# A graph network kernel on one core: the first message step placed inside the building of the adjacency

## The reference

```python
def gnn(node_feats, W1, b1, W2, b2, W_ih, b_ih, W_hh, b_hh, src, dst):   # 3125 nodes, 256 features
    for _ in range(6):                                                   # NUM_STEPS
        h = relu(node_feats @ W1.T + b1) @ W2.T + b2
        msg = segment_sum(h[src], dst, num_segments=3125)                # 53125 edges, sorted by dst
        gx = msg @ W_ih.T + b_ih
        gh = node_feats @ W_hh.T + b_hh
        xr, xz, xn = split(gx, 3); hr, hz, hn = split(gh, 3)
        r = sigmoid(xr + hr); z = sigmoid(xz + hz); n = tanh(xn + r * hn)
        node_feats = (1 - z) * n + z * node_feats
    return node_feats

def reference(x, src, dst, ...):
    x = x + gnn(layernorm(x), ...)
    x = x + ffn(layernorm(x))            # 8 experts, top 2 by gate, 256 -> 512 -> 256
    return x
```

## Time and profile before

| | us |
|---|---|
| median of 3 runs (2141.41 to 2143.67) | 2142.3 |
| the profiled execution | 2137.68 |
| its span | 2135.8 |
| preparation, 0 to the first build instruction | 129.2 |
| build, seven turns | 129.2 to 333.4 |
| flag, eleven relu sums, entry of the step loop | 333.4 to 371.7 |
| the rest of step 0, to the first message matmul of step 1 | 371.7 to 626.1 |
| steps 1 to 5 and the last stage | 626.1 to 2135.8 |

### The profile page before, as it was taken

How to read it: one execution, slowest core, us unless ns; L and a number is a source line. 1 busy time by engine, 2 the same in 40 slices (tenths; PEclk the granted TensorE clock), 3 DMA queues, 4 the chain that set the end, 5 groups by cost and what they waited for, 6 DMA issues and landing times.

```text
span 2135.8 us, 31987 instructions
## 1 busy us (share of the span) xinstructions
PE 1899.5 (89%) x11128; PEld 1125.1 (53%) x11129; DVE 1108.7 (52%) x2621; ACT 598.2 (28%) x1297; POOL 346.7 (16%) x454
## 2 busy tenths in 40 slices
PE   1666766999999999999999999999999999947996
PEld 1533334444564456544574445644466455637996
DVE  6579993245443445334452344524453355654775
ACT  0145553112221222221232122312222111215664
POOL 1012224555000000000000000000000011342665
PEclk7679998999999999999999999999999999968998
DMA  9910003443000000000000000000000010293543
GB/s 271 336 29 0 0 0 131 139 143 124 1 2 1 1 1 1 2 1 1 1 1 2 1 1 1 2 1 1 1 1 1 3 36 33 80 368 61 84 72 58
DMA packets 73647, 106.08 MB, mean 50 GB/s; under 512 B 11742, under 2 KB 64777, under 8 KB 72484
## 3 DMA queue, kind: packets, MB, share of 16 engines
q1 hardware_dynamic: 50238, 46.09, 7.1%
q0 software_dynamic: 18368, 38.09, 7.0%
q10 hardware_dynamic: 4902, 20.01, 2.4%
HBM read 43.59 MB, written 61.77 MB: 49 GB/s over the span
## 4 chain that ended last, share of the span: by engine, by line
PE 63%; issue 14%; DVE 13%; POOL 7%; ACT 1%; ACTq 0%; POOLq 0%; DMA 0%; SPq 0%; DVEq 0%
PE bank L1398 33%; PE bank L1422 23%; DVE hot_key L757 6%; PE bank L1382 4%; POOL out L559 3%; DVE hot_row L751 2%; POOL slot_in L536 2%; POOL tick L558 1%; PE bank L1377 1%; PE bank L1296 1%; PE bank L1324 0%; DVE r_lo L817 0%; PE bank L1270 0%; DVE st L643 0%; DVE xa L678 0%
## 5 line engine op out<-in xcount | busy, mean ns | idle before, releaser
L1398 PE MATMUL bank<-adj,r_hi 128*128 128x512 fp8e4 (+2 forms) x2100 | 730.9, 353 | 0.0
L1398 PE MATMUL bank<-adj,r_lo 128*128 128x512 fp8e4 (+2 forms) x2100 | 730.8, 353 | 0.0
L1398 PEld LDWEIGHTS bank<-adj,r_hi 128*128 128x128 f16 x2100 | 205.9, 98 | 190.0 <-issue 1.9
L1398 PEld LDWEIGHTS bank<-adj,r_lo 128*128 128x128 f16 x2100 | 205.7, 98 | 189.8 <-issue 1.8
L824 DVE SCALAR_TENSOR_TENSOR m_lo<-bank,msg_unit,m_hi 128x512 f16<-128x512 f32 (+2 forms) x84 | 57.2, 682 | 304.6 <-ACT m_hi L1109 304.6
L1324 PE MATMUL bank<-hot_key,hot_row 128*128 128x400 f16 x588 | 139.0, 351 | 60.5 <-DVE hot_key L757 58.1
L523 POOL MEMSET x_rows<- 128x4 f32 (+1 forms) x3 | 0.2, 98 | 1126.4 <-PE bank L1499 1126.4
L1422 PE MATMUL bank<-m_hi,wct_hi 128*128 128x512 f16 (+2 forms) x504 | 177.3, 352 | 0.0
L1422 PE MATMUL bank<-m_lo,wct_hi 128*128 128x512 f16 (+2 forms) x504 | 177.3, 352 | 0.0
L1422 PE MATMUL bank<-m_hi,wct_lo 128*128 128x512 f16 (+2 forms) x504 | 177.3, 352 | 0.0
L1422 PE MATMUL bank<-x_hi,wht_lo 128*128 128x512 f16 (+2 forms) x504 | 177.3, 352 | 0.0
(11 more groups left out here) (295 smaller groups left out, 3011.2 us busy)
## 6 DMA issues: line engine op xcount, KB each, us to landing
slot_in<-fill_rows SPq DMA_DIRECT2D x2, 13520.0 KB, 69.1
ffn_scratch<-pair POOLq DMA_DIRECT2D x32, 512.0 KB, 3.2
ffn_w<-ffn_scratch ACTq DMA_DIRECT2D x8, 2048.0 KB, 19.3
x_rows<-in_L_ffn_W POOLq DMA_DIRECT2D x32, 256.0 KB, 3.9
slot_x<-slot_in SPq DMA_DIRECT2D x30, 260.0 KB, 3.3
xa<-in_x SPq DMA_DIRECT2D x1, 3072.0 KB
x<-in_x ACTq DMA_DIRECT2D x1, 3072.0 KB
out<-x SPq DMA_DIRECT2D x4, 512.0 KB
```

Source lines behind the costliest of these rows:

```text
L1398: last = mm(bank[f][:, 0:n], r[:, q, f * P:(f + 1) * P], c, start=q == 0 and i == 0, stop=q == NT - 1 and i == len(todo) - 1)
```

## The change

The build loop is written out in full on all engines, and step 0 is worked beside it: window w of step 0 is now turn w's 448 columns (the last has 438). While turn w+1 is built, PE also runs the messages of window w; while turn w+2 is built, the gates of window w. The relu sums of step 0 stand in turns 0 and 1. To have banks for this, the slices use two banks (`RING` = 2) instead of four, and the degree sums take a place in the same ring. The 196 small matmuls of line 1328, the register work of the loop and the copies of `turn_key` go; DVE waits on `slice_full` itself. The window 5 gates, window 6 and eleven relu sums of step 1 follow the build, and the flag is read behind them. If the flag is set, x is restored and step 0 is done again with the exact counts; for that SP writes `x_hi` and `x_lo` to DRAM (2 x 1.6 MB, `x_kept`) before ACT's first eviction may run. In the preparation the slot sums come right behind `picked`, ahead of the weights; six parts of x stand ahead of the combined weights and seven between the eight groups of turned weights.

```diff
-RING = 4
+RING = 2
+X_EARLY = 6
+TURN_COLS = GROUP * SW
+FUSED_COL = [w * TURN_COLS for w in range(NW)]
+FUSED_LEN = [min(TURN_COLS, N + N % 2 - c) for c in FUSED_COL]
+CHUNK_Q = (0, 4, 8, 12, 16, 19, 22, NT)
@@ SP
+            sp.wait_ge(sem("state_lo"), NW)
+            for i, half_x in enumerate((x_hi, x_lo)):
+                sp.dma_start(x_kept[i], half_x[:].rearrange("p t n -> p (t n)")).then_inc(sem("x_kept"), 16)
@@ DVE: gate_op(s, w, f, k) is one of the nine gate operations
+            def beside(w, b):
+                if w == -1 and b % 3 == 1 and b >= 4:
+                    relu_lo(b // 3 - 1, b // 3 - 1, first=True)
...
+                if w >= 1 and b == 2:
+                    msg_lo(FIRST, w - 1, 1)
+                if w >= 2 and b == 3:
+                    state_lo(FIRST, w - 2)
+                if w >= 0 and b == 17:
+                    msg_lo(FIRST, w, 0)
+                for f, places in enumerate(((6, 8, 9, 10, 10, 13, 13, 14, 14), (18, 20, 21, 22, 22, 25, 25, 26, 26))):
+                    if w >= 1 and b in places:
+                        for k in range(GATE_OPS):
+                            if places[k] == b:
+                                gate_op(FIRST, w - 1, f, k)
+            for g in range(NSL):
+                hots(g)
...
+                beside(g // GROUP - 1, g % GROUP)
@@ ACT
+            act.wait_ge(sem("x_kept"), 32)
+            for g in range(NSL):
+                evict(g)
+                beside(g // GROUP - 1, g % GROUP)
@@ PE
+            def beside(w, b):
+                if w == -1 and b % 3 == 0 and b // 3 < RELU_BUILD:
+                    relu_sum(FIRST, b // 3)
+                if w == 0 and b in (0, 2, 4, 6):
+                    relu_sum(FIRST, RELU_BUILD + b // 2)
+                for f, places in enumerate(((2, 4, 5, 6), (14, 16, 17, 18))):
+                    if w >= 1 and b in places:
+                        gate_sum(FIRST, w - 1, f, places.index(b))
+                for f in range(DT):
+                    c = b - 7 - 12 * f
+                    if w >= 0 and 0 <= c < 7:
+                        messages(FIRST, w, f, CHUNK_Q[c], CHUNK_Q[c + 1], False)
+
+            for g in range(NSL):
+                slice_sums(g)
+                beside(g // GROUP - 1, g % GROUP)
+                if g % GROUP == GROUP - 1:
+                    degree_sums(g // GROUP)
+            gates(FIRST, NW - 2, 0)
+            messages(FIRST, NW - 1, 0, 0, NT, False)
+            gates(FIRST, NW - 2, 1)
+            messages(FIRST, NW - 1, 1, 0, NT, False)
...
+            for u in range(FUSED_A):
+                relu_sum(SECOND, u)
+            gates(FIRST, NW - 1, 0)
+            for u in range(FUSED_A, FUSED_B):
+                relu_sum(SECOND, u)
+            gates(FIRST, NW - 1, 1)
+            for u in range(FUSED_B, FILL_B):
+                relu_sum(SECOND, u)
             slow = read_slow_flag(pe)
...
-                with pe.Fori(0, LAST) as s:
+                with pe.Fori(1, LAST) as s:
```

More of the change, by code:

```diff
@@ L862, in state_lo @@
[L862 to L870 removed]
+                v.memset(small[:, 1:2], 0.0).then_inc(sem("re_gate_ops"), LEAD)
+                for u in range(USES):
+                    relu_lo(u, u, "re_")
@@ L871, in _ @@
+                for u in range(FILL_B):
+                    relu_lo(USES + u, u, "re_")
+            v.memset(small[:, 0:1], 0.0).then_inc(sem("build_over"), 1)
+            with dve.Fori(1, LAST) as s:
                 for u in range(FILL_B, USES):
@@ L1081, in _ @@
+            gates(FIRST, NW - 1, 1)
+            state_hi(FIRST, NW - 1)
+            for u in range(FUSED_B, FILL_B):
+                relu_hi(USES + u, u)
             slow = read_slow_flag(act)
@@ new lines, in messages @@
+            def messages(s, w, f, q0, q1, exact, again=""):
+                n, c0 = columns_of(s, w, again)
+                fused = s is FIRST and not again
+                if fused and q0 == 0:
+                    pe.wait_ge(sem("stage_free"), GROUP // 2 * (w + 1))
+                    if w:
+                        pe.wait_ge(sem("msg_lo"), half(s, w - 1, f) + 1)
+                if fused and w == 0:
+                    pe.wait_ge(sem("relu_lo"), (q1 + 1) // 2)
+                if not fused and w == 1 and f == 0:
+                    pe.wait_ge(sem(again + "msg_lo"), half(s, 0, 0) + 1)
+                    mm(bank[0][:, 0:2], ones_h[:], b1_rows[:, 0:2], start=True, stop=True)
+                if exact:
+                    pe.wait_ge(sem("planes_in"), (s + 1) * (32 * NW) + 32 * (w + 1))
+                for q in range(q0, q1):
+                    counts = [planes[:, i, q, 0:n] for i in range(2)] if exact else [adj[:, q, c0:c0 + n]]
+                    todo = [(r, c) for c in counts for r in (r_hi, r_lo)]
+                    for i, (r, c) in enumerate(todo):
+                        last = mm(bank[f][:, 0:n], r[:, q, f * P:(f + 1) * P], c,
+                                  start=q == 0 and i == 0, stop=q == NT - 1 and i == len(todo) - 1)
+                if q1 == NT:
+                    last.then_inc(sem(again + "msg_sums"), 1)
@@ new lines, in gates, with slice_sums @@
+            def gates(s, w, f, again=""):
+                for k in range(4):
+                    gate_sum(s, w, f, k, again)
+            def slice_sums(g):
+                i, b = divmod(g, GROUP)
+                ring_free(pe, g + i)
+                pe.wait_ge(sem("hots_full"), g + 1)
+                for s in range(SLOTS):
+                    k = (b % DEEP) * SLOTS + s
+                    last = mm(bank[2 + (g + i) % RING][:, 0:NT * SW], hot_row[b // 2 % 2][:, b % 2, s, :], hot_key[k][:], start=s == 0, stop=s == SLOTS - 1)
+                last.then_inc(sem("slice_full"), 1)
```

597 lines of the change are left out of this document (352 added, 245 removed).

## The result

| | before | after |
|---|---|---|
| median of 4 runs (lowest to highest), us | 2141.86 (2140.48 to 2143.67) | 2045.05 (2044.29 to 2045.87) |
| profiled execution: time, span, us | 2137.7, 2135.8 | 2045.75, 2043.7 |
| PE busy, share of the span | 89% | 91% |

The ratio is 0.9548 [0.9531, 0.9564], 96.8 us less by the medians. 2050 was forecast, 5 us too much.

What follows compares the result with a forecast made beforehand. DVE was taken to bound the build and PE the steps. Step 1 moving from 626.1 to 534.4 saves 91.7 us: 2137.7 becomes 2046.0, plus 4.6 for the median, said as 2050; range 2033 to 2072, chance 0.68.

Steps and rivals of the forecast that it cites:

- What bounds each stage, and that a step's matmuls fit beside the build: DVE bounds a build turn (28.7 of 29.0 us), PE a step (250 of 254), so step matmuls fit beside the build.
- Unit prices: Costs per operation: a 448-column matmul 0.189 us, a relu sum 1.5, a DVE gate operation 0.62 to 0.70, an eviction 0.49.
- Slot sums early: Preparation: slot sums right behind `picked` end at 64 us, DVE reaches its wait at 63.8, so they cost nothing there.
- State of x: Preparation: `state_lo` done at 111 us instead of 128.7, with 6 us for seven interleaved parts; ends 105 and 118.
- Copy of x: Before ACT's first eviction: queue held by the fill until 111, 10.5 us of copy, there at 124; ends 120 and 132.
- Turn 0 and 1: First two build turns: PE ends the first at 156.5 us, the second at 197.5, with 39.1 of matmuls and 2 more.
- rival 1: Fused turns: DVE's in-order waits cost 10 us a turn, making a turn 57 us and the result 2085; chance 0.18.
- Turns 2 to 6: Fused turns: PE paces with 47.4 us, stalls 1.7 at the turn's seam and 0.9 elsewhere, 50 a turn; ends 47.4 and 55.
- Tail: From the last slice to step 1: gates, messages, relu sums, last `state_lo`, then 4.6 and 6.8 us of branch; 84.1 us.
- Clock at the start of step 1: At step 1's start: 7 us without PE work make the clock fall again, costing 2.8 us.
- The sum: Whole kernel: step 1 starts 91.7 us earlier, so 2046.0 us profiled; 4.6 more for the median, stated as 2050.
- The clock in the fused turns: Fused turns: a quarter of PE's work at half speed makes a turn 50 + 12 us, 2110 in all; chance 0.05.

Runs made afterwards that it cites:

- TensorE's extra work: Changed kernel with the twelve 448-column matmuls of the first gate sum run twice in each of turns 2 to 6: 2053.4 us, ratio 0.9591.
- the kernel without any jump: Changed kernel with TensorE's program lacking the flag, the redo of step 0 and the steps with exact counts: 2050.2 us, ratio 0.9576.
- the kernel that jumps early: Changed kernel with TensorE reading the flag and jumping over the redo before step 1's eleventh relu sum, not behind it: 2043.1 us, ratio 0.9542.

## Why the prediction was right, step by step

- **What bounds each stage, and that a step's matmuls fit beside the build:** right, and shown from both sides (2.26 of 2.27 us for TensorE's extra work, nothing for DVE's).
- **Unit prices:** right; 448 columns at 0.189 gave 2.27 and the turn grew by 2.26.
- **Slot sums early:** 64 forecast, 64.0 measured; DVE waited 0.5 us for them.
- **State of x:** 111 forecast, 105.35 measured. The term that was mis-sized is the seven interleaved parts, 6 us. From the combined weights to the last part it took 22.1 us (83.2 to 105.35) where the block alone had taken 20.1: the parts cost 2. The other 1.8 us are in what stands ahead (83.2 against 85.0). It cost the forecast nothing, because the copy lands no earlier.
- **Copy of x:** first eviction forecast at 124, measured at 123.6, for the reason given: the fill held the queue (to 112, forecast 111). The bytes went at 420 to 440 GB/s, not at 311, and landing took some 3.5 us (from about 120 to 123.4) where 2 were allowed for issue and landing together: two errors that cancelled, so the 0.4 us are luck.
- **Turn 0 and 1:** ends at 156.5 and 197.5 forecast, 156.7 and 199.7 measured; turn 1 was 2.0 us under-priced (43.0 against 41). Its matmuls are the 39.1 worked out, and PE stood for 3.9 us: 2.6 in the middle, where 2 were forecast, and the rest at its first slices and before its degree sums, for which nothing was set. In the middle PE waited 1.9 us for `hot_key`, which stood on DVE behind `m_lo`, which had waited 1.3 us for ScalarE's `m_hi`. That is rival 1's mechanism, once and small.
- **Turns 2 to 6:** 50 forecast, 48.84 measured, 5.8 us in all. The matmuls are the 47.4 worked out plus 0.5; stalls were priced at 2.6 (1.7 at the seam, 0.9 for the rest) and are 0.9 to 1 in all.
- **Tail:** 84.1 forecast, 82.4 measured (443.9 to 526.3), but made of other parts. The step that failed is the branch: I added the 4.6 us of the flag and the 6.8 of the loop entry from the earlier trace rows as two separate delays. With no work between them they are one, 6.3 us, as the kernel without any jump shows. Against that, up to the last `state_lo` it took 2 us more, and the eleventh sum 3.1 instead of 1.8 us, each of its 256-column matmuls 0.21 apart as at 1.2 GHz. Most of the 2 us has the same cause, which the forecast set at nothing here: behind a wait of 2.4 us for `r_lo` a whole relu sum ran at half the clock, 3.0 us instead of 1.5 (the window below).
- **Clock at the start of step 1:** 2.8 forecast, 2.0 measured (24.5 us to the mark where it was 22.5), granted clock 0.91 in that stretch. In the kernel that jumps early it is 1.00 there, and the stretch takes 22.5.
- **The sum:** steps 1 to 5 would start 91.7 us earlier, with step 1's loss in it; they did so by 97.8. The 6 us are the seam (5.8 us), the double jump (5.1) and the clock (0.8), less turn 0 (0.2), turn 1 (2.0) and what the tail took more before the jump (3.4). The profile's last stage then took 5.6 more than before, by scatter, and hid most of it; the medians show it. The working's 2046.0 for the profiled execution, where 2045.75 was measured, is therefore luck. The 4.6 us put on top of it for the median had no ground in the new kernel: its median lies 0.7 us under its profiled execution.
- **Rivals.** In-order waits (a turn of 57 us): fell for turns 2 to 6, with DVE at 42 of 49 us and 4 us more of work for nothing. The clock in the fused turns: 1.00 granted in all of them. PE stands for only 0.9 us of 49 there. But the reason given against it, that short waits had not brought the clock to half in the build before, was misread: the 0.94 of the earlier trace rows is one stretch of 3.4 us at half the clock, at 319.4, and there are three more in the build, at 145.3, 203.4 and 261.4. PE stands there for 0.6 us before every second slice, and for 1.3 us, waiting for `hot_key`, just before or at each fall. First that stretch, then the one in the new kernel's tail:

```profile
319.40:322.80 3.40, 3.14 (x13) 1.51 (x14) 3.40 (x13) 1.02 (x6) 0.37 (x1) 0.50 0.00 0
499.80:503.20 3.40, 3.21 (x15) 2.24 (x16) 0.73 (x2) 0.01 (x1) 0.00 (x0) 0.50 0.00 0
```

The Trainium skill (TensorE: Matmul & The Clock Gate, "A second HAM failure mode: psum-queue depth-cycling") describes a clock that rises and falls where PE idles shortly between groups of matmuls. The build before agrees with it, at a ring of four banks; turns 2 to 6, at a ring of two but with PE full, show none of it. The two builds differ in how full PE is as well as in the ring, and no run tests the two apart. Serialised handoffs and a set flag: not seen.

The rule on branches of the Trainium skill (Runtime: NRT & Kernel Launch, "Instruction fetch mechanics") I had read as "only a taken branch to far code stalls, the sum is the same". The runs show more: 16 instructions behind the jump a second stall may come, or at the sixth, or none. The same section says that instructions lie in two lines that are filled in order; a loop that starts shortly before the end of such a line would behave so. The traces agree: one transfer of 16.4 KB for every 255 instructions, and each second stall ends 1.2 to 1.5 us after one has landed.

What stays open: the last stage, from the mark of step 5 to the end, took 483.6 to 490.8 us in the profiles, though all these kernels do the same there; I haven't found what it depends on. What the second stall costs a step (1.4, 2.3 or 4.5 us) adds up: from matmul to matmul over the stall, less the usual 0.216, it is 1.6, 2.0 or 2.6 us; the first stall at the jump back, 1.3 to 2.0 us from matmul to matmul in these kernels, is 0.2 shorter, 0.3 longer or 0.2 longer than in the profile of the changed kernel beside it; and without flag and redo 3.4 us at half the clock add 1.7. Why the first stall varies isn't known.

## What to carry to other kernels

A wait on a transfer belongs before the first instruction that would overwrite its source, and a transfer's start is read from what its queue still has to move, not from when its data are ready. When two stages with opposite bounds are fused, price the turn by the engine that is full in both and check it by adding a known amount of work to each engine. After any edit to the bounding engine's program, compare the time per iteration of its loops: a few instructions ahead of a loop can cost or give back as much as the edit was meant to bring.

## What the runs showed of the hardware that I had not expected

- 28 instructions ahead of a loop, executed once, cost 10 us (2051.0 against 2041.1). 20 in the kernel that jumps early gave back 5 us by the ratios (0.9542 to 0.9519), 6.7 by the mark of step 5 (1554.4 to 1547.6).
- TensorE's instructions come in transfers of 16.4 KB, one for every 255 of its instructions (92 in the changed kernel). A second stall behind a jump ended 1.2 to 1.5 us after such a transfer had landed, in nine steps of nine.
- The granted clock fell to half for 3.4 us behind waits of PE of 1.3 us (319.4, before) and 2.4 us (499.8, after).
- A transfer held behind others in its queue holds its issuing engine too: the issue of 1.6 MB took 15.3 us at 92.8 and 2.5 at 105.4, both ending at about 108, and 0.34 ahead of the fill.
- 3.28 MB from SBUF to DRAM flowed at 420 to 440 GB/s where the fill before it had 335.
